# One bank for the weighted sums, four banks for scores, and TensorE's order worked out anew

## What is computed

```python
scores = einsum('bqhd,bkhd->bhqk', q, k) / sqrt(HD)
scores = where(causal, scores, min)
attn = softmax(scores, axis=-1)
ao = einsum('bhqk,bkhd->bqhd', attn, v).reshape(B, S, H * HD)
x = x + ao @ wo
...
x = x + 0.5 * ffn(layernorm(x)); x = x + attn(layernorm(x)); x = x + 0.5 * ffn(layernorm(x))
```

## Time and profile before

| | us |
|---|---|
| median of 3 runs | 1946.1 (1941.53 to 1951.43) |
| the profiled execution | 1951.96 |
| its span in the trace | 1950.3 |
| TensorE busy | 1719.3 |
| VectorE busy | 1374.7 |
| ScalarE busy | 1078.1 |

### The profile page before, as it was taken

How to read it: one execution, slowest core, us unless ns; L and a number is a source line. 1 busy time by engine, 2 the same in 40 slices (tenths; PEclk the granted TensorE clock), 3 DMA queues, 4 the chain that set the end, 5 groups by cost and what they waited for, 6 DMA issues and landing times. The chain is left out here.

```text
span 1950.3 us, 30148 instructions
## 1 busy us (share of the span) xinstructions
PE 1719.3 (88%) x10630; PEld 741.5 (38%) x10630; DVE 1374.7 (70%) x2705; ACT 1078.1 (55%) x2301; POOL 445.5 (23%) x491
## 2 busy tenths in 40 slices
PE   4899999999749947899999998579999999985896
PEld 2333333333246733333333332333333333324674
DVE  7889999975243338889989881488999998715333
ACT  3355766767504424456676768235566767761442
POOL 6300202011005647001101020350020111100564
PEclk9789999999859977899999999768999999995898
DMA  4500203200001134200202000241020010000113
GB/s 130 127 5 3 50 27 99 43 1 2 8 26 40 43 102 137 50 2 6 47 2 50 2 2 2 70 139 33 2 46 6 17 36 2 2 8 22 33 43 87
DMA packets 59432, 75.61 MB, mean 39 GB/s; under 512 B 9527, under 2 KB 52092, under 8 KB 57976
## 3 DMA queue, kind: packets, MB, share of 16 engines
q1 hardware_dynamic: 50056, 62.10, 12.4%
q0 software_dynamic: 4992, 9.32, 1.8%
q10 hardware_dynamic: 4224, 2.10, 0.4%
HBM read 52.97 MB, written 21.43 MB: 38 GB/s over the span
## 5 line engine op out<-in xcount | busy, mean ns | idle before, releaser
L744 ACT ACTIVATE probs<-ps 128x512 f32<-128x512 f32 (+3 forms) x1920 | 884.9, 541 | 497.2 <-PE ps L852 494.9
L595 DVE TENSOR_REDUCE mpart<-ps 128x1 f32<-128x512 f32 (+3 forms) x1680 | 1018.3, 666 | 119.1 <-PE ps L806 72.4
L806 PE MATMUL ps<-ka,qa 96*128 96x512 bf16 (+3 forms) x1920 | 669.7, 371 | 34.7 <-DMA ka<-ksplit 22.8
L852 PE MATMUL ps<-qa,ka 96*128 96x512 bf16 (+3 forms) x1920 | 632.0, 357 | 23.6 <-ACT probs L744 22.2
L865 PE MATMUL ps<-probs,vv 128*9 128x512 f32 (+3 forms) x3840 | 442.7, 533 | 1.8 <-POOL probs L693 1.8
L693 POOL TENSOR_SCALAR_AFFINE_SELECT probs<-probs 128x512 f32<-128x512 f32 x192 | 121.9, 635 | 1208.3 <-ACT probs L744 1208.3
L806 PEld LDWEIGHTS ps<-ka,qa 96*128 96x128 bf16 x1920 | 191.8, 100 | 463.0 <-DVE mpart L595 316.2
L852 PEld LDWEIGHTS ps<-qa,ka 96*128 96x128 bf16 x1920 | 183.5, 99 | 259.4 <-ACT probs L744 146.0
L809 PE MATMUL ps<-mask_rows,identb 128*128 128x128 bf16 x768 | 160.8, 234 | 0.0
L1186 DVE SCALAR_TENSOR_TENSOR probs<-probs,slot_w,ps 128x448 f32<-128x448 f32 x78 | 53.1, 680 | 119.1 <-PE ps L1115 119.1
L865 PEld LDWEIGHTS ps<-probs,vv 128*9 128x9 f32 x3840 | 57.3, 89 | 141.2 <-ACT probs L744 95.2
(11 more groups left out here) (163 smaller groups left out, 1085.2 us busy)
## 6 DMA issues: line engine op xcount, KB each, us to landing
qa<-qsplit SPq DMA_DIRECT2D x27, 384.0 KB
ka<-ksplit SPq DMA_DIRECT2D x27, 384.0 KB
probs<-rope SPq DMA_DIRECT2D x12, 512.0 KB, 6.6
qa<-qsplit SPq DMA_DIRECT2D x36, 96.0 KB
ka<-ksplit SPq DMA_DIRECT2D x36, 96.0 KB
qsplit<-arena SPq DMA_DIRECT2D x6, 384.0 KB, 3.1
ksplit<-arena SPq DMA_DIRECT2D x6, 384.0 KB, 2.8
tokens<-arena SPq DMA_DIRECT2D x2, 1024.0 KB, 5.1
```

The lines of the kernel that those rows point to most:

```text
L595: dve.tensor_reduce(mpart[:, j % MD, h0:h0 + some, qt, kc], ps[:, bank, 0:some * w].rearrange("p (h w) -> p h w", h=some), axis=AX.X, op=A ...
L744: act.activation(probs[:, s % 2, h, 0:n], ps[:, u % SB, 0:n], ACT.Exp, scale=SCALE).then_inc(probs_ready, 1)
L806: ins = pe.matmul(dst, qa[0:KROWS, b, h0 + k, tile * 128:(tile + 1) * 128], ka[0:KROWS, b, h0 + k, kc * CH:kc * CH + n], start=True, stop= ...
L852: pe.matmul(dst, ka[0:KROWS, b, h, kt * 128:(kt + 1) * 128], qa[0:KROWS, b, h, c * CH + q0:(c + 1) * CH], start=True, stop=True).then_inc( ...
```

## The change

Three constants and four expressions. SB becomes 4: scores use banks 0 to 3, fillers 4 to 6. The sums have bank SB + MB = 7 alone, whatever the chunk, so that the first values block of a chunk now waits until ScalarE has copied the sums of the chunk just before it. In `core_schedule` a values block is taken to last 4 * n / 2.4 + 200 rather than + 60, the copy 600 rather than 480, and the new wait is in it (`sums_copied`). From these three the list of events comes out another. What is computed, and how many instructions of each kind there are, stays.

```diff
-SB, MB = 3, 3
+SB, MB = 4, 3
...
+    sums_copied = 0.0
...
-            main(exp_at[HPG * s - 1] + hop + masking, 4 * n / 2.4 + 60, min(j, len(chunks) - 1))
+            main(max(exp_at[HPG * s - 1] + hop + masking, sums_copied if pk == 0 else 0.0), 4 * n / 2.4 + 200,
+                 min(j, len(chunks) - 1))
...
-                act = max(act, pe + hop) + 480
+                act = max(act, pe + hop) + 600
+                sums_copied = act + hop
...
-                        act.activation(otf[:, j % 2, :], ps[:, 6 + j % 2, :], ACT.Copy).then_inc(output_copied, 1)
+                        act.activation(otf[:, j % 2, :], ps[:, SB + MB, :], ACT.Copy).then_inc(output_copied, 1)
...
-                        if kt == 0 and j >= 2:
-                            pe.wait_ge(output_copied, j - 1)
+                        if kt == 0 and j >= 1:
+                            pe.wait_ge(output_copied, j)
...
-                            ins = pe.matmul(ps[32 * h:32 * h + HD + 1, 6 + j % 2, q0:CH],
+                            ins = pe.matmul(ps[32 * h:32 * h + HD + 1, SB + MB, q0:CH],
```

## The result

The changed kernel takes 1918.4 us (median of 4 runs, 1916.2 to 1920.3) where the kernel before takes 1946.9: a ratio of 0.985, 95% interval 0.983 to 0.987, so 28.5 us saved. I had said 1924, 22 us saved. Beside it once more on another chip, where the kernel before takes 1969.1, the ratio was 0.983 (0.980 to 0.986).

A forecast was written before the change was run, and what follows sets the result against it. TensorE bounds the middle; in the end TensorE and ScalarE hand over at the third bank. Per layer 6.1 + 0.6 + 0.7 + 1.0 + 0.4 - 0.2 - 1.3 = 7.3; three layers 22 us, median 1924, range 1910 to 1940.

The forecast's parts named there:

- the plain steps: Chunks 14 and 15, steps of four score matmuls: 1.96 us each, a gain of 0.48 a step.
- The slack of 0.03 in the handing over: Plain steps: after a step's last exponential, the next could start at +1.81 us, ScalarE's turn for it being +1.84.
- rival (a): Plain steps: TensorE and ScalarE still wait on each other, leaking 0.25 us a round; 8 us gained, time 1938; chance 0.12.
- The diagonal: Masked steps ending chunks 14 and 15: values blocks wait for GpSimd's mask, the new bound; some 0.6 us a layer gained.
- The boundary: Chunk 14 to 15: copy and turning of the sums put the first values block at +2.7 us; 0.2 lost a layer.
- the cover of 1.1 us: Middle chunks: the copy of the sums ends at +1.36 us, the next values block comes at +2.50; cost put at nothing.
- The few-filler steps: Three steps like the step of six gain 0.7 us a layer; four without a rowmax in chunks 7 and 11, 1.0.
- another order neither gains nor loses: Middle of a layer: TensorE is the bound with the same matmuls, so the new order changes the time by nothing.
- The bursts: Reductions ahead of the maxout in chunks 0 to 2, lengthened by the planned 200: 0.4, 0.8, 0.1 us, 1.3 lost a layer.
- (b): Rival: in the middle the sums' copy comes too late for the next values block; at 1.0 us late, 1969; chance 0.04.
- (c): Rival: slow clock behind all three bursts makes them cost more, 16 us in all, time 1940; chance 0.06.
- (d): Rival: all waits for exponentials of scores vanish, masked steps too, bursts cost nothing; 40 us gained, time 1906; chance 0.08.

The follow-up runs named there:

- short_masks: Changed kernel with the causal mask on GpSimd cut to 8 of 128 columns: 1932.0 us, ratio 0.982 to the kernel before, on a slower chip.
- one_sums_bank: Kernel before with one bank for the sums, three for scores and its old order: 1964.8 us, ratio 0.9996 to the kernel before, on a slower chip.
- four_planned_60: Changed kernel with a values block planned at 60 rather than 200: 1935.4 us, ratio 0.984 to the kernel before, on a slower chip.
- start_as_before: Changed kernel, its planner reckoning with three score banks for chunks 0 to 2: 1929.7 us, ratio 0.980 to the kernel before; changed kernel beside it 1935.6.

## Why the prediction was right, point by point

**The bound, and the plain steps: right.** 1.96 us forecast, 1.96 measured in 9 of 9 steps from chunk 15's third on. The slack of 0.03 in the handing over held, so rival (a) did not come.

**The diagonal: right.** Forecast with the mask as the new bound: 7.45 from the last plain block to chunk 14's last, measured 7.37; 6.8 at the end of chunk 15, measured 6.7 (503.73 to 510.42). The boundary, 2.7, measured 2.77 (477.96 to 480.73). short_masks shows that it is the mask. For chunks 14 and 15 I had 6.9 a layer; 7.5 came.

**One bank for the sums: right in the sum, wrong in the reason's size.** It costs nothing with three banks for scores (one_sums_bank), and with four no values block waits for the copy. But the cover of 1.1 us that I read from the earlier trace rows is not there for the copy, since the turning wants it first. Had I looked for who else waits on `output_copied`, I would have seen that the turning follows the copy's end by 0.15 us.

**The few-filler steps and "another order neither gains nor loses": mis-sized.** This is where most of the 7 us are that I missed. For chunks 4 to 13 I had 1.7 a layer, counted at seven steps, and zero for the rest. Measured: 4.0. Before, 27 of the 92 steps counted there lose 0.04 to 0.12 us, 2.0 together, and 13 lose more, 4.0 together. After it is 4 and 5 steps, with 0.2 and 1.5. One such step, in chunk 9 (a block of 384 columns, two scores of 256 ahead of it), before and then after:

```profile
340.47 0.43 PE L852 MATMUL ps<-qa,ka 96*128 96x256 bf16 x2
340.83 0.83 PE L865 MATMUL ps<-probs,vv 128*9 128x384 f32 x8
```

```profile
340.04 0.38 PE L855 MATMUL ps<-qa,ka 96*128 96x256 bf16 x2
340.35 0.83 PE L868 MATMUL ps<-probs,vv 128*9 128x384 f32 x8
```

From the first of the two scores to the block it is 0.36 us before and 0.31 after. Where two scores stand in a row with three banks, the second starts 0.05 us late, below what the view marks as idle; that it waits for a bank is inferred, from the four banks under which it no longer does. The larger waits in these chunks are for the most part at masked blocks and at the turning of the sums. I had read a middle with 296.1 of 298 us busy as free of waits, and the busy time had hidden them; the prediction itself warned of that and then checked one step only.

**The bursts: right size, in part by luck, and the wrong cause.** 1.3 a layer forecast; chunks 0 to 3 went from 24.2 to 25.8 in the mean of the layers, 1.6. The steps that hold the bursts wait 0.4, 0.8 and 0.4 us longer, where I had 0.4, 0.8 and 0.1. Besides, the steps behind the bursts lose 0.6 more, which I had at nothing, and the other steps of these chunks 0.7 less, which I had not counted either; that the two cancel is luck. The cause was the plan's fourth bank (four_planned_60).

**The sum.** A layer: 7.5 for chunks 14 and 15, 4.0 for 4 to 13, 1.6 against: 9.9, three times 29.6, against 29.5 in the trace. Mine was 6.9 + 1.7 - 1.3 = 7.3.

**Rivals.** (b) is shut out by the trace of the changed kernel (one_sums_bank has three banks for scores, and cannot speak on it): at every boundary of layer 0 the copy ends 0.5 us or more ahead of the next chunk's first values block, and in the list of waits no values block (L868) waits for the copy (L754). (c) happened in part, with the sign that I had named for it. Behind the first burst, in layer 0 only, two steps take 4.07 and 3.71 us at a price of 2.4; behind the third burst, in all three layers, the first step takes 4.1 to 4.2, at a price of 1.6 each. Behind the second burst the changed kernel loses 1.5 a layer less than the one before, so that in the sum of the three layers it loses only 1.9 us more behind the bursts. (d) was right that the middle gives more, though its 2.6 for it was still short of 4.0, and wrong on the diagonal, where waits are left.

## What to carry to other kernels

Where one engine is in order and two others feed it, look at the start times of its instructions, not at its busy share; subtract what the instructions need, for every step and not for one, and small waits of a twentieth of a microsecond show up as a sum. A buffer that is held only for a hand-over can be taken from two to one if another wait already stands in front of its next use, and what it frees is worth most where the steps have nothing else to fill a wait. An order that was worked out for one number of buffers is not the best for another: with too few buffers the new one cost, and with four it was worth as much in the middle as the buffer. But look at all parts of it: in the sum it gave 1.1 us of 29.5, until the start was planned apart (start_as_before).

## What the hardware showed

The granted clock behind a burst was not the same from layer to layer or kernel to kernel. TensorE waits in the bursts for reductions; what comes next begins at 1.2 or at 2.4 GHz. The same place, behind the burst of chunk 0 in layer 0, in the changed kernel and then before (columns as above):

```profile
87.50:92.10 4.60, 4.60 (x24) 1.79 (x26) 2.50 (x4) 3.26 (x6) 0.00 (x0) 0.50 0.74 157
```

```profile
87.50:90.50 3.00, 3.00 (x26) 1.37 (x28) 2.74 (x5) 2.94 (x7) 0.00 (x0) 0.99 0.72 147
```

In the changed kernel chunk 1 waits and loses 10.8 us in layer 0 and 8.4 in the other two, in both of its profiled executions, though the three run one and the same list. A slow stretch also stands behind the third burst, at the first step of chunk 3, and in the changed kernel in all three layers. Layer 0, the changed kernel, then start_as_before, which has the same row of matmuls in this step (columns as above).

```profile
164.59:168.74 4.15, 4.15 (x28) 2.30 (x27) 2.65 (x7) 3.19 (x6) 0.00 (x0) 0.58 0.02 3
```

```profile
161.89:164.42 2.53, 2.53 (x27) 1.58 (x27) 2.36 (x7) 2.53 (x6) 0.00 (x0) 1.00 0.00 0
```

4.15 us at a mean granted clock of 0.58 and 2.53 at 1.00: 1.6 us, three times in the execution. In the kernel before it is chunk 2 that begins slowly, with steps of 4.50 and 3.38 us in layer 0. These differences are of the order of the gain that I tried to measure with start_as_before, and 3 to 5 of the 9 to 11 us by which its attentions are shorter stand in such steps. That was read in the rows; no run changed the clock alone.
